# Fused adapter and FFN layers: the first group's weight is made during the mixing, and part of its low words on GpSimd

## The reference

```
xt      = per sequence: W_cond[index].T @ x            # 64 x 64, mixes the tokens of a sequence
x       = x + xt @ W_base.T + b_base
            + 0.5 * irfft-matrix(sum over 3 adapters of (coef*mask) @ enc) applied to xt
gate,up = x @ W.T + 0.5 * low-rank terms picked by a second index    # 1024 -> 2752
down    = (silu(gate) * up) @ W_down.T + its low-rank term           # 2752 -> 1024
x       = x + down @ sign(W_ffn).T + bias
```

## Time and profile before

| what | value |
|---|---|
| median of three runs | 1940.96 us |
| the profiled execution | 1939.93 us |
| its span, first to last instruction | 1938.2 us |
| PE busy | 1912.8 us, 99% |
| DVE busy | 1493.0 us, 77% |
| ACT busy | 763.3 us, 39% |
| POOL busy | 543.9 us, 28% |
| mean granted PE clock | 0.998 |

### The profile page before, as it was taken

One profiled execution on the slowest core, in us unless ns is written; L12 is line 12 of the kernel. 1 busy time (PEld: TensorE's weight loads), 2 busy tenths in 40 slices (PEclk: granted clock), 3 DMA queues, 4 the chain that ended last, 5 costly groups with the idle time before them and its releaser, 6 DMA issues.

```text
span 1938.2 us, 31467 instructions
## 1 busy us (share of the span) xinstructions
PE 1912.8 (99%) x9088; PEld 1605.7 (83%) x9088; DVE 1493.0 (77%) x2484; ACT 763.3 (39%) x1450; POOL 543.9 (28%) x935
## 2 busy tenths in 40 slices
PE   6999999999999999999999999999999999999998
PEld 5888888888988888888898888888889888888887
DVE  6977777778778777777777877777877787777786
ACT  3453333334344343333344434333335443334331
POOL 6442222213415212211523322212071322222100
PEclk9999999999999999999999999999999999999999
DMA  9675445543476554444447655454334655555411
GB/s 245 152 147 108 103 98 116 121 94 82 126 149 127 106 115 100 101 99 88 119 116 143 124 113 110 106 116 99 70 102 131 139 121 110 121 110 113 99 44 44
DMA packets 320629, 219.43 MB, mean 113 GB/s; under 512 B 177192, under 2 KB 311208, under 8 KB 320544
## 3 DMA queue, kind: packets, MB, share of 16 engines
q1 hardware_dynamic: 281952, 189.47, 43.5%
q0 software_dynamic: 36352, 24.19, 7.0%
q10 hardware_dynamic: 2240, 4.72, 0.7%
HBM read 205.40 MB, written 12.58 MB: 112 GB/s over the span
## 4 chain that ended last, share of the span: by engine, by line
PE 92%; DVE 4%; issue 2%; ACT 2%; DMA 0%; POOLq 0%; DVEq 0%; ACTq 0%; POOL 0%
PE ps L1404 26%; PE ps L1406 26%; PE ps L1405 26%; PE ps L1611 6%; PE ps L1538 2%; PE ps L1458 2%; PE ps L1459 2%; DVE ps L876 2%; PE ps L1430 1%; PE ps L1477 1%; PE ps L1428 1%; DVE split L862 1%; ACT split L608 0%; ACT hidden L608 0%; PE ps L1648 0%
## 5 line engine op out<-in xcount | busy, mean ns | idle before, releaser
L1404 PE MATMUL ps<-x,split 128*128 128x512 f32 x1376 | 537.7, 391 | 1.3 <-DVE split L862 1.3
L1406 PE MATMUL ps<-x,split 128*128 128x512 f32 x1376 | 536.3, 390 | 0.0
L1405 PE MATMUL ps<-x,split 128*128 128x512 f32 x1376 | 535.4, 389 | 0.0
L608 ACT ACTIVATE split<-ps 128x512 fp32r<-128x512 f32 x344 | 203.0, 599 | 450.8 <-DVE ps L876 438.8
L505 POOL DMA_DIRECT2D nat_ad<-L_cond_A_down x224 | 137.3, 620 | 733.4 <-DVE ps L876 724.3
L1406 PEld LDWEIGHTS ps<-x,split 128*128 128x128 f32 x1376 | 258.3, 188 | 55.8
L1405 PEld LDWEIGHTS ps<-x,split 128*128 128x128 f32 x1376 | 258.4, 188 | 54.8
L1404 PEld LDWEIGHTS ps<-x,split 128*128 128x128 f32 x1376 | 259.0, 188 | 50.0 <-DVE split L862 2.5
L1404 PE MATMUL ps<-hidden 128*128 128x512 f32 x672 | 261.5, 389 | 0.0
L1405 PE MATMUL ps<-hidden 128*128 128x512 f32 x672 | 261.5, 389 | 0.0
L1406 PE MATMUL ps<-hidden 128*128 128x512 f32 x672 | 261.4, 389 | 0.0
(11 more groups left out here) (137 smaller groups left out, 2830.5 us busy)
## 6 DMA issues: line engine op xcount, KB each, us to landing
nat<-L_cond_W_gate SPq DMA_DIRECT2D x336, 128.0 KB
nat<-L_cond_W_up SPq DMA_DIRECT2D x336, 128.0 KB
nat_down<-L_cond_W_down SPq DMA_DIRECT2D x112, 384.0 KB, 6.4
nat_a<-L_ffn_weight SPq DMA_DIRECT2D x128, 128.0 KB, 2.8
nat<-effective_weight SPq DMA_DIRECT2D x24, 512.0 KB
nat<-x SPq DMA_DIRECT2D x16, 512.0 KB
nat_b<-L_cond_B_gate POOLq DMA_DIRECT2D x224, 24.0 KB, 2.2
nat_b<-L_cond_B_up POOLq DMA_DIRECT2D x224, 24.0 KB, 2.1
```

The costliest lines, as they stand in the source:

```text
L608: act.activation(dst, src, func).then_inc(piece_hi, 1)
L1404: pe.matmul(dst, a[0], b[0], start=first, stop=False)
L1405: pe.matmul(dst, a[0], b[1], start=False, stop=False)
L1406: return pe.matmul(dst, a[1], b[0], start=False, stop=last)
```

## The change

All edits are in the first group.

- **Order of loads.** SP loads enc and the table ahead of x block 3, b_base ahead of base tiles 4 to 7. POOL reads only four of the eight mixing indices ahead of the first gathers, and gathers A_gate only after base tile 1 is transposed.
- **A smaller product.** A quarter of the fourier table is loaded (its columns 0 to 255). `low_rank_product` has 12 products of 256 columns where 8 of 512 stood, and stands before mixing step 3 where it stood before step 6. The sums and differences that give the other three quarters are made on DVE in `low_rank_words`, for 96 columns of each quarter first, and for the other 160 later.
- **Work moved to ACT.** `wsum`, its negative, the high words of enc and half of the product's way out of PSUM.
- **Tiles made one by one.** `make_weights` makes tile 0 alone before mixing step 5, then pairs (1, 2), (3, 4), (5, 6), and 7 alone. Tiles 0 and 1 are added and split in halves of 512 columns.
- **Low words on GpSimd.** Tiles 3 to 7 get their low words by `made_low` on POOL: 3 and 4 after the B gathers, 5, 6 and 7 between the gathers of `load_rest`.
- **Pieces in another order.** The B tiles go after tile 7 (`FIRST_HEAD`, `FIRST_BESIDE`), ahead of BREM and `ranks`.

```diff
+FIRST_HEAD = (["AG"] * 2 + ["AU"] * 2 + ["REM"] * 2 + ["G0"] * 2 + ["B"] * 3 + ["BREM"] + ["U0"] * 2
+              + ["G1"] * 2 + ["ADREM"])
...
+FIRST_BESIDE = {u: BESIDE[u] for u in range(3, 7)}
+MADE = ((0,), (1, 2), (3, 4), (5, 6), (7,))
...
             def load_rest(index, making=False):
                 for b, i in enumerate(index):
+                    if making and b % 2 == 0 and b < 6:
+                        made_low(5 + b // 2)
...
+            def made_low(u):
+                s = (SPLIT_W + u) % SPLIT_SLOTS
+                wait(plain_hi, 4 + u + 1)
+                pool.wait_ge(plain_lo, 4 + u)
+                pool.tensor_tensor(split[:, s, 1, :], base_t[:, u], split[:, s, 0, :].bitcast(F32), ALU.subtract)\
+                    .then_inc(plain_lo, 1)
...
+                if g == 0:
+                    wait(base_turned, 2)
                 wait(piece_lo, START + LOW_PIECES * g)
                 load_a(index, A_gate, 0)
                 wait(piece_turned, PIECES * g)
                 load_a(index, A_up, 1)
                 load_b(index, 0)
-                load_rest(index)
+                if g == 0:
+                    for u in range(3, 5):
+                        made_low(u)
+                load_rest(index, g == 0)
...
-            index = chosen(cond_index, 0)
+            index = chosen(cond_index, 0, slice(0, 4))
             pool.wait_ge(const_set, 1)
-            for p in range(4):
+            for p in range(2):
+                load_cond(index, p)
+            index = [None] * 4 + list(chosen(cond_index, 0, slice(4, GB)))
+            for p in range(2, 4):
                 load_cond(index, p)
...
+            def low_rank_words(i):
+                cols = LOW_COLUMNS[i]
+                moved = enc.rearrange("r (q c) -> r q c", q=4)
+                even, odd = even_sums[:, :, cols], moved[:, 2:4, cols]
+                whole, words = (t.rearrange("r (q c) -> r q c", q=4) for t in (low_rank, low_s))
+                dve.wait_ge(g_moved, 2)
+                dve.tensor_tensor(even[:, 0], moved[:, 0, cols], moved[:, 1, cols], ALU.add)
+                dve.tensor_tensor(even[:, 1], moved[:, 0, cols], moved[:, 1, cols], ALU.subtract).then_inc(low_step, 1)
+                dve.wait_ge(low_step, 4 * i + 1)
+                dve.tensor_tensor(whole[:, 0:2, cols], even, odd, ALU.add)
+                dve.tensor_tensor(whole[:, 2:4, cols], even, odd, ALU.subtract).then_inc(low_step, 1)
+                dve.wait_ge(low_step, 4 * i + 2)
+                dve.tensor_copy(words[:, :, cols], whole[:, :, cols]).then_inc(low_step, 1)
+                dve.wait_ge(low_step, 4 * i + 3)
+                dve.scalar_tensor_tensor(out=words[:, :, cols], in0=words[:, :, cols].bitcast(F32),
+                                         scalar=own_sb[0:STACK, GB + 1:GB + 2], in1=whole[:, :, cols], op0=ALU.mult,
+                                         op1=ALU.add).then_inc(low_step, 1)
...
+            def first_layer_first():
+                for u in range(KC):
+                    x1_total(0, u)
+                    if u < 5:
+                        add_weight(3 + u)
+                    if u < 4:
+                        turn_base(4 + u)
+                    beside_turn(0, u)
+                    dve.wait_ge(base_turned, min(KC, 5 + u))
+                    x1_low(0, u)
+                    beside_lows(0, u)
+                lora_b_tiles(0, 0, "B", 0)
+                lora_b_rest(0)
...
             def mixing_all(g, before=None, making=False):
                 for e in range(8):
-                    if e == 6 and making:
+                    if e == 3 and making:
                         low_rank_product()
+                    if e == 5 and making:
+                        make_weights(0)
                     mixing(g, e, before)
```

More of the change, by code:

```diff
@@ L263, in _, with column @@
         def _(sp):
[L264 to L269, removed]
+            def column(dst, src, done):
+                for hq in range(4):
+                    with nc.allow_non_contiguous_dma(reason="1024 words, once"):
+                        sp.dma_start(dst[32 * hq:32 * hq + 32, :], src.rearrange("(q k h) -> q h k", q=4, k=KC)[hq])\
+                          .then_inc(done, 16)
             base_rows = W_base.rearrange("(oq u oo) (hq c) -> u hq oo oq c", oq=4, u=KC, hq=4)
@@ new lines, in mixing_first @@
+            def mixing_first():
+                for p in range(2):
+                    plain_unit(0, p, NAT_X + p, SPLIT_X + p)
+                for p in range(2):
+                    cond(0, p)
+                plain_unit(0, 2, NAT_X + 2, SPLIT_X + 2)
+                act.wait_ge(enc_in, 96)
+                copy(enc_s.rearrange("r k (q d) -> r q k d", q=4),
+                     enc.rearrange("r (q k d) -> r q k d", q=4, k=KC)).then_inc(enc_step, 1)
+                mixing(0, 0)
+                low_rank_weights()
+                mixing(0, 1)
+                cond(0, 2)
+                plain_unit(0, 3, NAT_X + 3, SPLIT_X + 3)
+                mixing(0, 2)
+                act.wait_ge(enc_step, 2)
+                act.wait_ge(g_psum, 1)
+                copy(enc[:, 0:512], ps[0:STACK, 6, :]).then_inc(g_moved, 1)
+                mixing(0, 3)
+                cond(0, 3)
+                for e in range(4, 6):
+                    mixing(0, e)
+                made_halves(0)
+                for e in range(6, 8):
+                    mixing(0, e)
+                store_weight(0)
+                made_halves(1)
+                store_weight(1)
+                made_unit(2)
+                store_weight(2)
@@ L1255, in add_weight @@
             def add_weight(u):
+                v, n = MADE_OF[u]
                 dve.wait_ge(base_turned, u + 1)
[L1257 removed]
+                dve.wait_ge(w_psum, v + 1)
                 tile = base_t[:, u].rearrange("p (k o) -> p k o", k=KC)
[L1259 to L1271 removed]
@@ new lines, in enc_words @@
+            def enc_words():
+                low = own_sb[0:STACK, GB:GB + 1]
+                dst = enc_s.rearrange("r k (q d) -> r q k d", q=4)
+                src = enc.rearrange("r (q k d) -> r q k d", q=4, k=KC)
+                dve.wait_ge(enc_step, 1)
+                for q in range(4):
+                    last = dve.scalar_tensor_tensor(out=dst[:, q], in0=dst[:, q].bitcast(F32), scalar=low, in1=src[:, q],
+                                                    op0=ALU.mult, op1=ALU.add)
+                last.then_inc(enc_step, 1)
@@ new lines, in mixing_first @@
+            def mixing_first():
+                for p in range(2):
+                    plain_unit(0, p, NAT_X + p, SPLIT_X + p)
+                for p in range(2):
+                    cond(0, p)
+                plain_unit(0, 2, NAT_X + 2, SPLIT_X + 2)
+                adapter_sum()
+                mixing(0, 0)
+                enc_words()
+                mixing(0, 1)
+                cond(0, 2)
+                plain_unit(0, 3, NAT_X + 3, SPLIT_X + 3)
+                mixing(0, 2)
+                turn_base(0)
+                turn_base(1)
+                low_rank_out()
+                low_rank_words(0)
+                mixing(0, 3)
+                cond(0, 3)
+                mixing(0, 4)
+                add_weight(0)
+                mixing(0, 5)
+                made_low_half(0, 0)
+                mixing(0, 6)
+                made_low_half(0, 1)
+                mixing(0, 7)
@@ L1435, in first_layer @@
                 m = SPLIT_W + u
-                pe.wait_ge(plain_lo, 12 * g + 4 + u + 1)
+                by_halves = g == 0 and u < 2
+                if not by_halves:
+                    pe.wait_ge(plain_lo, 12 * g + 4 + u + 1)
                 if half == 0:
@@ L1731, in shape_constants @@
     table[H - 1] = (1 - 2 * (n % 2)) / np.sqrt(H)
-    table = table[:, 0:H // 2]
+    table = table[:, 0:H // 4]
     row = np.arange(P)
```

313 lines of the change are left out of this document (161 added, 152 removed).

## The result

The changed kernel takes 1950.38 us (median of 6 runs, 1948.33 to 1952.71) against 1940.89 (1940.17 to 1941.30): ratio 1.005, 95% interval 1.0039 to 1.006. It is 9.5 us slower; 1938.9 had been forecast, with a range up to 1944.0. Its profiled execution took 1950.81 us, 1949.1 of them span.

A forecast was written before the change was run, and what follows sets the result against it. PE was taken to bound the kernel, with 19 us of waits and its own work up to the ranks open to change. Ranks 5.5 us earlier less 3.5 for the B tiles gave 2.0 less: 1938.9 us, range 1935.2 to 1944.0.

The forecast's parts named there:

- the last sentence on the low words: Rest gathers on POOL: remaining 16 end near 88.5 us, memsets near 92, before they are needed at 97 to 98.
- Start: First gather and PE's first matmul: fewer index reads put that matmul at 11.15 us, 1.05 us won.
- Product: Low-rank product: twelve products of 256 columns in 5.2 us, running from 17.9 to 23.1 us.
- Words: Words low_s after the product: PE waits 1.4 us instead of 2.7; first layer starts near 32.
- POOL's subtraction: Low words on POOL: 2.25 us each, bounds 0.95 and 2.7; PE's waits give back 4.0 us.
- The clock: PE's clock at the first layer: no fall to 0.50 once the 3.8 us wait goes, 1.4 us won.
- The B tiles: Between tile 7's words and the ranks: three B tiles delay rank_sum, PE waits 3.5 us.
- The half clock after rank_sum: PE behind the rank_sum wait: the clock may fall, costing up to 1.5 us, kept inside the range.
- Words in time: Rival, POOL's low words: a subtraction costs 0.95 us, 3.3 us more won, 1935.6 us; chance 0.20.
- The start does not move: Rival, first gather: it lands at 11.4 us as before, total 1940.0 us; chance 0.05.
- POOL slower: Rival, POOL's subtractions: 2.0 us gain used up at about 2.8 each, 1943.8 us total at 3.5; chance 0.13.
- DVE and POOL shut each other out: Rival, two-operand SBUF operations: four subtractions each start 0.67 us later, total 1941.6 us; chance 0.17.

The follow-up runs named there:

- e1: Changed kernel with the 16 nat_b_rem gathers first and nat_ad after tile 7's subtraction, GpSimd subtractions kept: 1942.54 us, ratio 1.0009.
- e8: Changed kernel with SP's loads of the gate, up and down weights held until nat_b_rem is there: 1943.98 us, ratio 1.0016.
- e2: Changed kernel with the low words of tiles 3 to 7 on DVE, no subtractions on POOL: 1939.87 us, ratio 0.9996.
- e4: Kernel before with only the low words of tiles 3 to 7 moved to POOL, placed as in the changed kernel: 1953.10 us, ratio 1.0063.
- e10: e2 with POOL made to wait at three places for ACT's copies of x, so gathers are late without subtractions: 1944.77 us, ratio 1.0021.
- e6: e1 with the B tiles beside tiles 0 to 2 again, as in the kernel before: 1941.89 us, ratio 1.001.
- e7: e2 with the B tiles beside tiles 0 to 2 again, as in the kernel before: 1935.34 us, ratio 0.9974.
- e9: e7 with the low word of tile 4 alone made on POOL, before the rest gathers: 1935.42 us, ratio 0.9977.
- e3: Changed kernel with BREM's transposition, copies and low words behind the ranks, gathers unchanged: 1943.20 us, ratio 1.0012.
- e5: Changed kernel with 38 extra matmuls of 512 columns on PE before the first group's wait for rank_sum: 1949.12 us, ratio 1.0042.

## Why the prediction was wrong

**The step that failed** is the last sentence on the low words: "The remaining 16 gathers end near 88.5 and the memsets, 3.1, near 92, before they are asked for at 97 to 98." It priced issue at the rate of an undisturbed queue, counted no landing, and asked only when the memsets are needed. BREM's own rows, which DVE asks for at 96.7, come at 103.1. The gathers' issue ended at 97.1, 8.6 us later than said: tile 7's subtraction ended 3.7 later (82.5 instead of 78.8), and 5.2 are the stall. The landing adds 7.8. Rows that could have warned were in the trace of before. At the same place in the same list of gathers, at a DMA share of 0.29, POOL had already stopped for 2.3 us; and the gathers of L_cond_B_down (64 KB each, where these have 4), which stood at 82 to 100 us beside the same loads of SP, stopped it for 4.6 and 6.8 us at shares of 1.18 and 1.24 and landed in 6.3 at the median:

```profile
58.63 0.61 POOL L492 DMA_DIRECT2D nat_ad<-L_cond_A_down  x1 [2.31 <-issue]
...
89.36 2.34 POOL L481 DMA_DIRECT2D nat_a<-L_cond_B_down  x3 [4.61 <-issue]
...
98.49 1.57 POOL L481 DMA_DIRECT2D nat_a<-L_cond_B_down  x2 [6.79 <-issue]
```

The experiments show it: e1 (other order), e8 (no traffic) and e2 (no holding) remove the wait beyond 3.6 to 4.4 us; e4 makes a wait of 8.2 us out of this edit alone; e10 makes one of 9.8 us without a subtraction.

**The forecast's terms, one by one:**

- *Start, 11.15 forecast.* PE waited 11.8 us. Over the changed kernel and the nine of its variants the profiled wait is 11.1 to 12.5, so the size of this term is within what one execution shows.
- *Product.* It ran from 18.6 to 23.7, 5.1 us for the forecast 5.2, 0.7 late at its start.
- *Words.* Low words of low_s at 27.3, as forecast; the wait was 0.6 instead of 1.4, since PE came later. First layer from 32.5 (32.1 forecast): the weight product of 128 columns was put at 0.5 and takes 0.95 (27.34 to 28.29). Second half late by 0.25 (0.6).
- *POOL's subtraction.* 2.38 or 2.39 undisturbed, up to 2.82; 2.25 forecast. The price was near. The waits of PE were 2.60, 0.40 and 1.23 for 2.0, 0.5 and 1.5.
- *The clock.* "The gap of 2.7 did not do it by itself" was taken to mean that 2.0 at tile 3 would be safe. It was 2.60, and the clock fell to 0.50 for over 3 us (window 55 to 58). Nor do the rows of before carry that sentence. The wait of 2.73 ended at 36.34 and the one of 3.80 began at 37.54; the mean clock from 37 to 38 us is 0.81, so it fell near 37.6, when the second wait had hardly begun:

```profile
37.00:38.00 1.00, 0.53 (x5) 0.32 (x3) 0.74 (x2) 0.00 (x0) 0.94 (x3) 0.81 1.09 99
```

  In e1 the clock fell 0.8 us after the end of its 2.60 us wait, while PE was working, so the 2.73 may have brought it down by itself. From tile 3's start to the next weight product is 7.19 us here and 5.56 in e2, where PE waited 0.9 and the clock stayed: 1.6 us. This, 0.2 in the waits, 0.9 in the two weight products of 128 columns (0.5 forecast for each), and 0.3 in front of tile 5, where PE starts at 68.57, just behind the end of POOL's subtraction at 68.52, make 3.0 of the 3.3 us by which the ranks (88.16) are later than 84.9; the rest is in pieces too small to place.
- *The B tiles, 3.5 forecast.* rank_sum came 12.6 us after the sum starts in the forecast. In the trace it is 19.1 from 88.36 to 107.5; less DVE's 6.46 for nat_b_rem that is 12.7. e1 and e8, without the late rows, wait 3.6. This term was exact.
- *The half clock after rank_sum.* It was held to 1.5 us inside the range. After 10.0 us it cost 2.7, after 3.6 (e1) 1.6: the rest tile took 6.95 us.

Together: ranks 3.3 later than forecast, 6.5 more waiting, 2.7 of clock: 12.5 us, of the 12.9 between 1937.9 and 1950.81.

**The rivals.** *Words in time* did not happen. *The start does not move*: 11.8 us stands between the 12.2 of before and the 11.15 forecast, inside the spread of the executions. *POOL slower* named the right side, but not the mechanism: the subtractions were 2.4 to 2.8, at most at the 2.8 it called harmless. *DVE and POOL shut each other out* is shown, in both directions. When POOL reads first, DVE's low word of x waits until POOL is through; when DVE starts first, POOL's subtraction is longer by a little less than what is left of DVE's operation. Timelines of DVE and of POOL of the changed kernel:

```profile
65.56 0.69 DVE L946 TENSOR_TENSOR x<-acc,x 128x512 fp32r<-128x512 f32 x1
...
81.30 1.80 DVE L946 TENSOR_TENSOR x<-acc,x 128x512 fp32r<-128x512 f32 x1
```

```profile
65.70 2.82 POOL L537 TENSOR_TENSOR split<-base_t,split 128x1024 fp32r<-128x1024 f32 x1 [7.34 <-ACT split L622]
```

At 80.16 POOL began (2.38, to 82.54), DVE's operation of 81.30 ended at 83.10, 0.56 after it. At 65.56 DVE began, and POOL, 0.14 later, took 2.82 for 2.38. By the rule that these two engines exclude each other on such operations (the Trainium skill, SBUF — State Buffer, Who interferes with whom), the trace agrees. I had priced it at 2.7 us if it hit every tile; it made one word of x 1.1 us longer and three subtractions 0.3 to 0.4. (In e4 and e6 more of DVE's low words of x fall into a subtraction, and seven of them take 1.1 to 2.9 us.) PE was waiting for tile 3's directly. Tile 5's counts too: PE starts that tile 0.05 us behind its end, and POOL has no gap from there to the end of tile 7's subtraction (65.70 to 82.54), so its 0.4 us are in the waits for tiles 6 and 7.

## What to carry to other kernels

When work is put in front of a gather, price the gather to its landing and to whoever takes it, not only its issue; and look for what other queues will be doing at its new time. A row of "issue" in front of a gather in the trace of before is a warning, above all where it stands beside the loads that the moved gather will meet. Before giving work to GpSimd because it is idle, compare the critical chain: 2.4 us on it against 1.2 on DVE lengthened a chain that PE was waiting for, and with all low words on DVE and the B tiles where they had been, the other edits brought the 5.5 us of e7.

## What the runs showed of the hardware

- **A gather issued on GpSimd stops longer in its issue beside the traffic of other queues.** The same gather, the eighth of the last sixteen of the rest rows, stopped POOL for 1.2 us in e7 and 1.6 in e8 (mean DMA share during the stop 0.08 and 0.09), 2.3 in the kernel before (0.29), 2.2 in e9 (0.73), 5.2 in the changed kernel (1.29), 5.5 in e4 (1.29) and 5.7 in e10 (1.16). The share during the stop does not decide alone: in e2 it was 1.2 us at 0.97, nearly all of that traffic in the last microsecond, behind 4 us at 0.13. In every kernel with this order of gathers the stop is at this one, whether it is issued at 59 or at 95 us; in e1 and e6, with the other order, the long stop (6.9 and 6.8 us, at 1.24) is at the last of the 32. What sets the place was not tried.
- **The length of a gap alone does not decide on the clock.** In the changed kernel, 2.60 us of waiting at tile 3 were followed by 0.50. In e6 the wait at the same tile was 2.78 and the clock stayed at 1.00:

```profile
54.53 0.50 PE L1538 MATMUL ps<-turned,split 128*128 128x512 f32 x1 [2.78 <-POOL split L549]
```

```profile
55.00:58.00 3.00, 3.00 (x15) 2.48 (x14) 3.00 (x5) 1.96 (x3) 0.52 (x1) 1.00 0.31 127
```

  The five kernels with a wait of 2.6 there (e1, e3, e5, e8 and the changed one) fell to 0.50. In the same way, waits for low_s of 1.17 us in e1, 1.24 in e5 and 1.65 in e10 were followed by 0.50 between 28.9 and 34.1 us, and one of 1.53 in e7 was not. What tells these apart was not tried and stays open. Such a fall moved the first layer's start to 34.07 in e5, where the changed kernel has 32.53 with the same start of the product in front (27.33 and 27.34): 1.5 us, so single executions of one kernel can differ by it.
